# Graph attention and a routed FFN: the prologue reordered, GpSimd on one row tile in four, projections over four pairs of PSUM banks

## The reference

```
xn  = layernorm(x);  Wh = xn @ W;  s = Wh @ a[:256];  t = Wh @ a[256:]
e   = leaky_relu(s[:, None] + t[None, :], 0.2), masked where adj is 0
x   = x + softmax(e, axis=1) @ Wh
y   = layernorm(x);  probs = softmax(y @ Wr + br);  top 2 of 8 experts, weights normalised
x   = x + sum over the two experts of weight * (gelu(ln(y)*g_e+b_e @ W1_e + b1_e) @ W2_e + b2_e)
```

## Time and profile before

| | us |
|---|---|
| median of 3 executions | 1014.33 |
| lowest and highest | 1012.05, 1014.99 |
| the profiled execution | 1008.72 |
| its span from first to last instruction | 1006.9 |
| TensorE, VectorE, GpSimd, ScalarE busy in the span | 949.3, 787.5, 640.0, 613.8 |

### The profile page before, as it was taken

How to read it: one execution, slowest core, us unless ns; L and a number is a source line. 1 busy time by engine, 2 the same in 40 slices (tenths; PEclk the granted TensorE clock), 3 DMA queues, 4 the chain that set the end, 5 groups by cost and what they waited for, 6 DMA issues and landing times. The chain is left out here.

```text
span 1006.9 us, 22940 instructions
## 1 busy us (share of the span) xinstructions
PE 949.3 (94%) x7550; PEld 797.3 (79%) x7551; DVE 787.5 (78%) x1197; ACT 613.8 (61%) x886; POOL 640.0 (64%) x640
## 2 busy tenths in 40 slices
PE   3877999999999999999999999999999999999994
PEld 2766998998889988889888887777777777777762
DVE  6476999999999999999999546688566567667653
ACT  2757889888888788887878444433433343343441
POOL 6602224257485874865827548888888888888652
PEclk9999999999999999999999999999999999999998
DMA  8635788778878888687886887353333232233221
GB/s 272 127 116 136 218 300 212 242 226 250 284 214 258 249 245 291 199 275 240 232 271 190 306 340 281 56 149 64 50 54 60 42 52 53 42 47 49 41 37 21
DMA packets 92236, 170.97 MB, mean 170 GB/s; under 512 B 19952, under 2 KB 69360, under 8 KB 83824
## 3 DMA queue, kind: packets, MB, share of 16 engines
q1 hardware_dynamic: 58384, 134.07, 40.0%
q0 software_dynamic: 24048, 26.23, 16.7%
q10 hardware_dynamic: 9712, 9.45, 3.3%
HBM read 136.91 MB, written 41.19 MB: 177 GB/s over the span
## 5 line engine op out<-in xcount | busy, mean ns | idle before, releaser
L1094 ACT ACTIVATE hf<-tp,b_cols 128x256 f32<-128x256 f32 (+1 forms) x312 | 116.3, 459 | 175.2 <-PE tp L864 172.7
L758 PE MATMUL acc<-wh,pt_hi 128*128 128x256 f16 x768 | 209.3, 273 | 0.0
L759 PE MATMUL acc<-wh,pt_hi 128*128 128x256 f16 x768 | 209.3, 273 | 0.0
L760 PE MATMUL acc<-wh,pt_lo 128*128 128x256 f16 x768 | 209.3, 273 | 0.0
L544 POOL TENSOR_TENSOR x_late<-x_late,wsp 128x1024 f32<-128x1024 f32 x32 | 79.3, 2479 | 179.7 <-DMA x_late<-in_L_ffn_W 174.1
L880 PE MATMUL acc<-w_sb,h_hi 128*128 x568 | 170.9, 379 | 5.1 <-issue 3.8
L1240 DVE SCALAR_TENSOR_TENSOR sc<-t_row,s_col 128x2048 f32<-128x2048 f32 x64 | 166.2, 2596 | 4.5 <-PE tp L742 4.4
L862 PE MATMUL tp<-x_hi,w_sb 128*128 128x256 f16 (+1 forms) x624 | 161.2, 264 | 1.9 <-ACT hf L1094 1.8
L650 POOL DMA_INDIRECT out<-y_sb,yidx x71 | 120.1, 1691 | 65.9 <-DVE y_sb L1561 33.4
L864 PE MATMUL tp<-x_down,w_sb 128*128 128x256 f16 (+1 forms) x624 | 161.3, 264 | 0.0
L863 PE MATMUL tp<-x_lo,w_sb 128*128 128x256 f16 (+1 forms) x624 | 160.8, 263 | 0.0
(11 more groups left out here) (223 smaller groups left out, 1784.8 us busy)
## 6 DMA issues: line engine op xcount, KB each, us to landing
adj_sb<-in_adj SPq DMA_DIRECT2D x64, 1024.0 KB, 7.0
x_late<-in_L_ffn_W SPq DMA_DIRECT2D x32, 512.0 KB, 9.7
wsplit_dram<-wsp SPq DMA_DIRECT2D x32, 512.0 KB, 8.4
w_sb<-wsplit_dram SPq DMA_DIRECT2D x32, 512.0 KB, 8.6
xs<-rows_dram ACTq DMA_DIRECT2D x32, 260.0 KB, 3.1
wsp<-in_L_ffn_W POOLq DMA_DIRECT2D x32, 256.0 KB, 4.9
x<-in_x SPq DMA_DIRECT2D x32, 128.0 KB, 9.9
out<-x SPq DMA_DIRECT2D x32, 128.0 KB
```

Of the source, the lines that this page charges most:

```text
L758: pe.matmul(o, pt_hi[g][:, cols], wh[:, j, 0, :], start=(j == 0), stop=False)
L759: pe.matmul(o, pt_hi[g][:, cols], wh[:, j, 1, :], start=False, stop=False)
L760: m = pe.matmul(o, pt_lo[g][:, cols], wh[:, j, 0, :], start=False, stop=False)
```

## The change

VectorE makes W @ a right after the first moments, and normalises tiles 2 and 3 ahead of the second moments. GpSimd normalises only tiles 1, 5, 9 and so on; VectorE takes the other three of four. The four pairs of banks `xt_ps`/`rt_ps`, `tp[0]`, `tp[1]` and `acc[0]`/`acc[1]` take the projections in turn, and a projection waits for the evacuation of the one four before. The last one is made inside the attention's first step, between its first two blocks of transposes. The first step's masks move behind the last row; those of row tile 1, the exponentials and the scores get other places between the evacuations.

```diff
+        side = (xt_ps, rt_ps)
+        def banks(j):
+            if j % 4 == 1 or j % 4 == 2:
+                b = tp[j % 4 - 1][:, :].rearrange("p (h n) -> p h n", h=2)
+                return [b[:, h, 0:D + 2] for h in range(2)], b
+            return [(side if j % 4 == 3 or j == 0 else acc)[h][:, 0:D + 2] for h in range(2)], None
...
 # GpSimd
-                for i in range(start + 1, start + n, 2):
-                    if i == start + n - 1 and m + 1 < len(batches):
-                        scales(m + 1)
+                for i in range(start + 1, start + n, 4):
                     normalise_x(i)
+                if m + 1 < len(batches):
+                    scales(m + 1)
...
 # TensorE, pair_t(p)
-                pe.wait_ge(s_xn, p + 1)
-                pe.wait_ge(s_xo, p + 1)
+                pe.wait_ge(s_xn, 3 * (p // 2) + 1 + 2 * (p % 2))
+                pe.wait_ge(s_xo, p // 2 + 1)
...
 # TensorE, project(j)
+                if j == 4:
+                    pe.wait_ge(s_tr, 2 * NP)
                 if j > 2:
-                    pe.wait_ge(s_whh, 2 * (j - 1))
-                    pe.wait_ge(s_whl, 2 * sum(lows[:j - 1]))
+                    pe.wait_ge(s_whh, max(2, 2 * (j - 3)))
+                    pe.wait_ge(s_whl, max(2, 2 * sum(lows[:j - 3])))
...
-            for j in range(1, NP):
+            for j in range(1, NP - 1):
                 project(j)
...
 # TensorE, p_transpose(i, u, g)
+                if g == 1 and i == 0:
+                    pe.wait_ge(s_whl, 2 * sum(lows[:NP - 1]))
+                    pe.wait_ge(s_whh, T - 2)
...
 # TensorE, av(i, u, g)
+                if g == 1 and i == 0:
+                    pe.wait_ge(s_whl, TS)
+                    pe.wait_ge(s_whh, T)
...
 # TensorE, attend(i)
                     p_transpose(i, u, 0)
+                    if i == 0:
+                        project(NP - 1)
                     p_transpose(i, u, 1)
...
-            pe.wait_ge(s_whl, TS)
-            pe.wait_ge(s_whh, T)
+            pe.wait_ge(s_whl, 2 * sum(lows[:NP - 2]))
+            pe.wait_ge(s_whh, T - 4)
             for i in range(T):
                 attend(i)
...
 # ScalarE, in the loop over pairs
                 if p == 6:
-                    wh_first()
-                if p == 8 or p == 12:
-                    mask(0, 0, p // 4 - 2)
+                    wh_hi(0)
...
 # ScalarE, attend(i)
                     p_hi(i, 0)
+                    if i == 0:
+                        wh_hi(NP - 1)
                     p_hi(i, 1)
...
-            for j in range(1, NP):
-                if j == 6 or j == 7:
-                    exps(0, 0, j - 6)
+            for j in range(1, NP - 1):
+                if j < 3:
+                    mask(0, 0, j - 1)
+                if j == 6:
+                    mask(1, 1, 0)
+                if j == 7:
+                    exps(0, 0, 0)
+                if j == 8:
+                    mask(1, 1, 1)
+                if j == 10:
+                    exps(0, 0, 1)
                 wh_hi(j)
-                if j == 4 or j == 7:
-                    mask(1, 1, j // 7)
...
 # VectorE, statistics and normalisation
             next_stats(0, 4)
             moments(0)
-            next_stats(4, 8)
+            project_a()
             dve.wait_ge(s_rstd, 1)
             dve.wait_ge(s_mean, 1)
             normalise(0)
-            project_a()
+            next_stats(4, 8)
+            normalise(2)
+            normalise(3)
             moments(1)
-            normalise(2)
             next_stats(8, 12)
...
             normalise(6)
+            normalise(7)
...
                 normalise(start + 2)
+                normalise(start + 3)
                 next_stats(start + 14, start + 16)
+                normalise(start + 4)
                 if m + 1 < len(batches):
                     moments(m + 1)
-                normalise(start + 4)
                 normalise(start + 6)
+                normalise(start + 7)
...
 # VectorE, after the last normalisation
-            lo_first()
+            wh_lo(0)
+            scores(0, 0, 0)
+            scores(0, 0, 1)
+            wh_lo(1)
             diagonal(0, 0)
-            scores(0, 0, 0)
-            wh_lo(1)
             wh_lo(2)
-            scores(0, 0, 1)
+            masked(0, 0)
             wh_lo(3)
-            masked(0, 0)
             wh_lo(6)
+            scores(1, 1, 0)
             wh_lo(7)
-            scores(1, 1, 0)
+            scores(1, 1, 1)
             wh_lo(8)
             wh_lo(9)
-            scores(1, 1, 1)
             diagonal(1, 1)
             masked(1, 1)
-            for j in range(12, NP):
+            for j in range(12, NP - 1):
                 wh_lo(j)
...
 # VectorE, attend(i)
                     p_lo(i, 0)
+                if i == 0:
+                    wh_lo(NP - 1)
```

More of the change, by code:

```diff
@@ L238, in build @@
         s_rstd = sem("rstd_done")
-        s_xn = sem("xn_even_done")
-        s_xo = sem("xn_odd_done")
+        s_xn = sem("xn_done")
+        s_xo = sem("xn_by_pool_done")
         s_xnt_ps = sem("xnt_in_psum")
@@ L710, in project @@
                     pe.wait_ge(s_xnt, T)
+                if j == 4:
+                    pe.wait_ge(s_tr, 2 * NP)
                 if j > 2:
-                    pe.wait_ge(s_whh, 2 * (j - 1))
-                    pe.wait_ge(s_whl, 2 * sum(lows[:j - 1]))
+                    pe.wait_ge(s_whh, max(2, 2 * (j - 3)))
+                    pe.wait_ge(s_whl, max(2, 2 * sum(lows[:j - 3])))
                 for h in range(2):
-                    o = (xt_ps, rt_ps)[h][:, 0:D + 2] if j == 0 else tp[j % 2][:, h * 512:h * 512 + D + 2]
+                    o = banks(j)[0][h]
                     for k in range(KD):
@@ L942, in wh_of @@
                 return wh32[:, n - TS:n - TS + 2, :] if n >= TS else wh[:, n:n + 2, 0, :]
[L944 to L949, removed]
             def wh_hi(j):
                 n = 2 * late_pairs[j]
-                ps = tp[j % 2][:, :].rearrange("p (h n) -> p h n", h=2)
+                single, both = banks(j)
                 act.wait_ge(s_wh, 2 * j + 2)
-                act.activation(s_col8[:, n:n + 2], ps[:, :, D], ACT.Copy, scale=SLOPE - 1.0)
-                act.activation(wh_of(n), ps[:, :, 0:D], ACT.Copy).then_inc(s_whh, 2)
+                if both is None:
+                    for h in range(2):
+                        act.activation(s_col8[:, n + h:n + h + 1], single[h][:, D:D + 1], ACT.Copy, scale=SLOPE - 1.0)
+                    for h in range(2):
+                        act.activation(wh_of(n)[:, h, :], single[h][:, 0:D], ACT.Copy).then_inc(s_whh, 1)
+                else:
+                    act.activation(s_col8[:, n:n + 2], both[:, :, D], ACT.Copy, scale=SLOPE - 1.0)
+                    act.activation(wh_of(n), both[:, :, 0:D], ACT.Copy).then_inc(s_whh, 2)
             act.wait_ge(s_ds, 1)
@@ L1208, in _ @@
                 normalise(start + 2)
+                normalise(start + 3)
                 next_stats(start + 14, start + 16)
+                normalise(start + 4)
                 if m + 1 < len(batches):
                     moments(m + 1)
-                normalise(start + 4)
                 normalise(start + 6)
+                normalise(start + 7)
             base = n[0]
             dve.wait_ge(s_par2, 16 * 5)
[L1217 to L1220, removed]
             def wh_lo(j):
                 n = 2 * late_pairs[j]
-                ps = tp[j % 2][:, :].rearrange("p (h n) -> p h n", h=2)
+                single, both = banks(j)
                 dve.wait_ge(s_whh, 2 * j + 2)
-                dve.tensor_tensor(wh[:, n:n + 2, 1, :], ps[:, :, 0:D], wh[:, n:n + 2, 0, :], ALU.subtract).then_inc(s_whl, 2)
+                if both is None:
+                    for h in range(2):
+                        dve.tensor_tensor(wh[:, n + h, 1, :], single[h][:, 0:D], wh[:, n + h, 0, :], ALU.subtract).then_inc(s_whl, 1)
+                else:
+                    dve.tensor_tensor(wh[:, n:n + 2, 1, :], both[:, :, 0:D], wh[:, n:n + 2, 0, :], ALU.subtract).then_inc(s_whl, 2)
             def scores(n, u, h):
```

## The result

The changed kernel took 999.57 us (median of 4 runs), the kernel before on the same chip 1013.25 (4 runs): a ratio of 0.985, 95% interval 0.982 to 0.989. One of the four runs took 1017.27 us at a mean granted clock of 0.944, and the ratio is made from the other three, 996.11 to 1001.02 with a median of 998.11. The profiled execution took 998.11 with a span of 996.3, where that of before took 1008.72 with 1006.9.

What follows compares the result with a forecast made beforehand. TensorE is busiest, so time must come from its waits, here ahead of tile 2. Pairs -6.3, projections -9.3, tile 0 +1.7, meetings +0.5 give -13.4 us against the median 1014.33: 1000.9, range 996.5 to 1006.

Steps and rivals of the forecast that it cites:

- meetings: Pairs: VectorE normalisations lengthened where GpSimd's are still running; 0.5 us added on the path, possibly 0 or 1.7.
- Part 1: Start: early W @ a puts first transposes at 10.6 and pair 2's at 15.95 instead of 20.10, 4.15 earlier.
- Part 2: TensorE's slow start: slow rate lasts for as much work as before, to 21.2; transposes 4 are the first fast ones.
- fast from the first matmul -2.6: Forecast's own bound at the start: TensorE at the fast rate from its first matmul would take off 2.6 us.
- Part 3: Pairs: GpSimd's pace gives way to TensorE's 1.30 a pair; they end at 39.8 instead of 46.14, -6.3 us.
- Part 4: Projections: 14 x 1.75 plus one wait of 1.2 at project(7); tile 0 at 65.5 instead of 81.12, -9.3 us.
- Rival (b): Projections stay tied to VectorE, two thirds of 7.3 us idle return: +4, some 1005; chance 0.08.
- Part 5: Tile 0: ScalarE limits its first part; project(15) ahead of the second block gives back 1.7 us; tile 2 near 95.3.
- rival (d): Start and pairs: TensorE stays at its slow rate; to the end of the pairs 17 us, 1018; chance 0.02.
- rival (c): Gain swallowed behind tile 2 by something on its own clock, such as loads: within 3 us of 1014.3; chance 0.02.

Runs made afterwards that it cites:

- after again: The changed kernel timed once more, unaltered, against the kernel before: 998.71 us, ratio 0.985.
- half to GpSimd: Changed kernel with W @ a early, but GpSimd normalising every second tile as before: 1003.18 us, ratio 0.993 to the kernel before.
- two deep: Changed kernel with four pairs of banks, but each projection waiting for the evacuation of the pair two before: 1005.58 us, ratio 0.993 to the kernel before.
- both and port: Changed kernel with project(15) behind tile 0's second block, p_hi(0,2) and p_hi(0,3) earlier, w_rest waiting for scores: 997.49 us, ratio 0.984 to the kernel before.
- Last behind: Changed kernel with project(NP - 1) behind tile 0's second block of transposes instead of ahead of it: 996.27 us, ratio 0.983 to the kernel before.
- pairs only: Kernel before with only the change's statistics, normalisations and shares (GpSimd one tile in four): 1008.73 us, ratio 0.996 to the kernel before.

## Why the prediction was right, and where it was off

**Right in sum.** 1000.9 was forecast and 999.57 measured, within the range. Part of the nearness is luck: my sum of -13.4 was put against the median of before, while the traces differ by only 10.6. By terms, from the traces: pairs with meetings -5.6, projections -9.3, tile 0 +1.7, the clock +2.1, behind tile 2 +0.5, together -10.6. The last term lies within scatter: in the two traces of the changed kernel the stretch from tile 2 to the last tile's last transposes alone took 474.6 and 477.1 us. The trace of before is a low one: of 39 further executions of that kernel, all but one took longer than its 1008.72 us. Where in the kernel they take it, no trace shows.

**Part 1, the start: 0.4 to 0.5 late.** First transposes at 11.04 (forecast 10.6), pair 2's at 16.46 (15.95). `project_a` began at 8.22, not 7.75, after waiting 0.5 for the load of `a`, and GpSimd's tile 1 took 1.64 instead of 1.25, ending 0.25 behind VectorE's `normalise(0)`. VectorE's and GpSimd's timelines after:

```profile
8.22 0.42 DVE L1167 CUSTOM_DVE_ANT_0 sc<-rows,sc 128x256 f32<-128x256 f32 x1 [0.50 <-DMA sc<-in_L_gnn_a]
...
19.82 0.41 DVE L1198 TENSOR_SCALAR rows<-sc 128x256 f32<-128x256 f32 x1 [0.56 <-POOL sc L520]
```

```profile
9.25 1.64 POOL L527 TENSOR_SCALAR rows<-sc 128x256 f32<-128x256 f32 x1 [0.18 <-POOL sc L520]
...
19.95 1.38 POOL L527 TENSOR_SCALAR rows<-sc 128x256 f32<-128x256 f32 x1 [0.17 <-issue]
```

**Part 2, the slow start: the number came true, the reason did not.** Pair 4's transposes stand at 21.43 (forecast 21.2), and in the trace after they are the first at the short length. But in seven traces with the same start pair 2's are short already, and pair 4's come no earlier. TensorE's timeline of "after again":

```profile
16.41 0.63 PE L699 MATMUL tp<-ident,rows 128*128 128x128 f32 x4 [0.97 <-issue]
...
18.27 0.66 PE L699 MATMUL tp<-ident,sc 128*128 128x128 f32 x4 [0.37 <-DVE sc L1198]
...
21.37 0.63 PE L699 MATMUL tp<-ident,rows 128*128 128x128 f32 x4 [1.58 <-issue]
```

Pair 4 needs GpSimd's tile 9, which ends at 19.95 + 1.38 = 21.33 (the last row under Part 1) and which my timetable left out. In the trace after the slow rate happened to last just as long and cost nothing. So the 21.2 was luck, and the bound "fast from the first matmul -2.6" was worth 0. That the rate rises after a like amount of matmuls was read from one row, and these traces do not bear it out. In "half to GpSimd", where TensorE stood 3.4 us ahead of pair 3, the granted clock was low until 24.5.

**Part 3, the pairs: E 40.58, forecast 39.8 plus 0.5 for meetings.** -5.6 instead of -5.8 with the meetings counted. The meetings themselves cost VectorE nothing (below). The 0.8 beyond 39.8 is 0.2 from the later pair 4, 0.3 lost at the row at 30.50, which waits for ScalarE's copy as its like did before at 33.01 and which my 1.30 a pair left out, and small gaps for the rest. That 0.5 for meetings nearly covered them is luck. From TensorE's timeline after:

```profile
30.50 1.13 PE L711 MATMUL acc<-wsp,sc 128*128 128x256 f32 x4 [0.18 <-ACT wsp L951]
```

The attribution was incomplete. I named GpSimd's share as the pace and the masks in passing; the experiments give 3.7 us at E to the share, 3.0 to the masks' place, and only 0.6 to the early W @ a when it stands alone. They don't add up to 5.6, because each is hidden while another limits: masks cost 1.3 in the old pairs and 3.0 in the new.

**Meetings.** In the trace after, VectorE's normalisations stayed at 0.40 to 0.42 us beside GpSimd's (the rows at 19.82 and 19.95). They do hold each other up elsewhere, for part of an instruction. In the trace of before six of VectorE's took 0.50 to 0.62; five of them began 0.7 to 0.9 us after one of GpSimd's and ended 0.15 behind its end, as 25.45 + 0.61 against 24.70 + 1.22. In the trace after it was GpSimd that lost: its normalisations of 1.64 and 1.47 both ended 0.25 behind VectorE's. The Trainium skill describes the lock as one under which the loser waits for the other's whole instruction (SBUF — State Buffer, section "SBUF: two separate sides"). In no trace did a normalisation on VectorE lose GpSimd's whole 1.22; for the two-input scores against `w_rest` the trace agrees with it to nearly the full length, 2.34 to 4.23 us and 2.13 to 4.07. The page's sentence binds the lock on VectorE's side to "two SBUF inputs" or a two-port mode. I weighed it without that condition, and whether a normalisation runs in such a mode no run shows.

**Part 4, the projections: right.** 25.71 us, forecast 25.7; one wait of 1.06 at 52.27, released by VectorE's evacuation behind `masked(0)` (forecast 1.2, near 50). The forecast's 14 x 1.75 + 1.2 is 25.7, not the 25.6 written there; the sum used 25.7. VectorE's timeline after: the masking and the evacuation it held back.

```profile
47.03 4.42 DVE L1274 CUSTOM_DVE_ANT_0 sc<-sc,bias_sb 128x4096 f32<-128x4096 f32 x1
...
51.37 0.42 DVE L1250 TENSOR_TENSOR wh<-xt_ps,wh 128x256 f16<-128x256 f32 x1
```

Rival (b) is what "two deep" built: with one iteration of cover instead of three 7.65 us return.

**Part 5, tile 0: right as far as it went.** `p_hi(0,1)` ends 4.73 after tile 0's start (forecast 4.7), and 10.57 later the second block begins (forecast 10.6). ScalarE's timeline after:

```profile
70.00 1.02 ACT L997 ACTIVATE pt_hi<-tp 128x1024 f16<-128x1024 f32 x1
```

The step that failed is the next sentence, tile 2 at 95.3: it took for granted that TensorE would run at the full rate from the second block on. The low clock had been weighed only for the start (rival (d)). My step for `project(15)` said that it "fills a wait of TensorE for `p_lo(0,0)`, which is not on this path"; it did, but that joined TensorE's idle time into one pause of 2.21 us, and a fall followed in five of seven traces. Why not in the other two is open.

**Behind tile 2: the gain was passed on**, as forecast against rival (c), for 11 us. But (c) returns with smaller sums: tile 2 at 93.5 instead of 97.7 gave nothing that the time shows clear of its scatter. The last block of transposes of the last tile comes 474 to 481 us after tile 2 in the fourteen traces, whatever was changed. Between the trace after (474.6) and "both and port" (477.9) the waits that differ are two; first those of after, then of "both and port", both for 100 to 590 us:

```profile
PE tp L755 <- ACT pt L997: 4.8, 6, 1.3
PE rt_ps L806 <- DVE oh L1358: 3.3, 4, 1.1
```

```profile
PE tp L757 <- ACT pt L999: 5.8, 6, 1.3
...
PE rt_ps L808 <- DVE oh L1366: 5.2, 5, 1.3
```

In the attention `rt_ps` takes the router's products. Why the stretch scatters is open.

**A better version?** "Last behind" has the lowest median (996.27), but its interval of the ratio (0.980 to 0.986) overlaps that of the changed kernel (0.983 to 0.987, timed again). I don't claim it.

## What to carry to other kernels

When a stage waits for evacuations that stand behind long operations on their engine, count the iterations between writing a bank and writing it again: three iterations of 1.75 us covered a masking of 4.42 but for 1.1, and with one iteration, in the same order of work, 6.0 us of waits stood. The depth with the old order of work was not run, so what the depth gives alone is not shown. Costs that hide each other must be taken out together: the masks in ScalarE's row cost 1.3 us beside slow pairs and 3.0 beside fast ones. Where an edit gathers TensorE's idle time into one pause of 2 us or more, carry a branch in which the next work runs at the low clock: here 1.3 to 3.0 us.

## What was not expected of the hardware

After a pause of 2.21 us the granted clock fell to 0.50 in five traces of seven, for 3.4 us in two and 6.8 in three. In the traces of before and of "pairs only" a pause of 2.34 us among the projections brought none, while pauses of 3.0 and 3.4 us elsewhere brought a fall of 3.4 each. The three falls of 6.8 us cost 2.1, 3.0 and 2.2 us (16.1, 16.95 and 16.2 from the second block to tile 2, against 13.99), the two of 3.4 us 1.3 and 1.7. 24 transposes that nobody reads filled the pause at no cost that the time shows. And the two-input scores of VectorE and `w_rest` of GpSimd make each other wait for nearly the whole of an instruction, while one-input normalisations of both overlap, at a cost to VectorE of 0.2 us or nothing.
